# Two buffers for layer 1's x, another interleaving of the last two periods, a flag in two parts, and early recurrent gate products in the last unit

## The reference

```python
# layer 0
mask = adj > 0
h  = relu((x @ W1a)[:, :, None, :] + (x[:, :, None, :] - x[:, None, :, :]) @ W1b + b1)
y  = einsum('bjkh,bjk->bjh', h, mask) @ W2 + mask.sum(-1)[..., None] * b2
x  = layernorm(x + y)
# layer 1
m   = relu(relu(x @ W1 + b1) @ W2 + b2)
msg = relu(einsum('bij,bjh->bih', adj, m))
gi, gh = msg @ W_ih.T + b_ih, x @ W_hh.T + b_hh      # parts r, z, n
r, z = sigmoid(i_r + h_r), sigmoid(i_z + h_z)
n   = tanh(i_n + r * h_n)
out = layernorm(x + (1 - z) * n + z * x)
```

## Time and profile before

| of the profiled execution | |
|---|---|
| its own time | 1053.67 us |
| span, first to last instruction | 1051.9 us |
| TensorE matmuls busy | 903.9 us, 86% |
| VectorE busy | 860.2 us, 82% |
| ScalarE busy | 558.1 us, 53% |
| GpSimd busy | 299.2 us, 28% |
| mean granted TensorE clock | 0.956 |

### The profile page before, as it was taken

The page is one execution under the profiler, slowest core; times in us unless marked ns, Lnnn a source line. Parts: engine busy times, 40 slices in busy tenths (PEclk is TensorE's granted clock), DMA queues, the critical chain, the costliest instruction groups (busy, mean ns, idle before and its releaser), DMA issues.

```text
span 1051.9 us, 24844 instructions
## 1 busy us (share of the span) xinstructions
PE 903.9 (86%) x10037; PEld 609.8 (58%) x10070; DVE 860.2 (82%) x1043; ACT 558.1 (53%) x1612; POOL 299.2 (28%) x285
## 2 busy tenths in 40 slices
PE   2778889989898998989898998989899898997854
PEld 1445656656666666556666665566666655664543
DVE  5489998888988889898889988898888989897531
ACT  3434454665655566564656566564556657453431
POOL 2111120423314151422315152331415142233230
PEclk9799999999999999999999999999999999999875
DMA  3131212112131211122121311213121212110000
GB/s 124 28 95 41 71 42 72 32 36 71 41 82 30 77 41 44 54 51 71 41 66 42 81 39 28 71 41 82 34 73 42 64 34 51 41 42 12 11 11 11
DMA packets 31425, 53.27 MB, mean 51 GB/s; under 512 B 8137, under 2 KB 16972, under 8 KB 31308
## 3 DMA queue, kind: packets, MB, share of 16 engines
q1 hardware_dynamic: 31308, 51.65, 19.1%
HBM read 13.87 MB, written 4.19 MB: 17 GB/s over the span
## 4 chain that ended last, share of the span: by engine, by line
PE 55%; ACT 16%; DVE 12%; issue 8%; POOL 4%; SPq 2%; another core or an unknown queue 1%; DMA 0%; POOLq 0%; DVEq 0%; ACTq 0%
PE PS L735 12%; PE PS L744 8%; DVE AC L1046 5%; PE PS L818 3%; ACT AM L1311 3%; PE PS L583 3%; PE PS L801 3%; DVE AC L1057 3%; PE PS L588 3%; ACT YO L1272 2%; POOL st L1417 2%; PE PS L609 2%; ACT AC L1358 2%; PE PS L721 2%; PE PS L575 2%
## 5 line engine op out<-in xcount | busy, mean ns | idle before, releaser
L1057 DVE SCALAR_TENSOR_TENSOR AC<-PS,AC 128x1152 f32<-128x1152 f32 (+1 forms) x288 | 351.7, 1221 | 79.9 <-PE PS L735 75.8
L1046 DVE SCALAR_TENSOR_TENSOR AC<-PS,AC 128x1152 f32<-128x1152 f32 (+1 forms) x288 | 351.2, 1220 | 66.5 <-PE PS L744 47.2
L735 PE MATMUL PS<-DM,VA 128*128 128x192 fp8e5 (+1 forms) x1152 | 136.8, 243 | 21.9 <-ACT AC L1358 8.4
L735 PE MATMUL PS<-DM,VB 128*128 128x192 fp8e5 (+1 forms) x1152 | 137.8, 244 | 0.0
L744 PE MATMUL PS<-DM,VB 128*64 128x192 fp8e5 (+1 forms) x1152 | 97.7, 250 | 41.7 <-DVE AC L1057 41.7
L735 PEld LDWEIGHTS PS<-DM,VA 128*128 128x128 f16 x1152 | 90.2, 100 | 54.4 <-issue 28.6
L744 PEld LDWEIGHTS PS<-DM,VB 128*64 128x64 f16 x1152 | 43.2, 110 | 119.6 <-issue 62.4
L1468 POOL MEMSET AC<- 128x768 f32 x32 | 23.7, 740 | 282.1 <-DVE DM L1027 267.3
L744 PE MATMUL PS<-DM,VA 128*64 128x192 fp8e5 (+1 forms) x1152 | 99.4, 254 | 0.0
L735 PEld LDWEIGHTS PS<-DM,VB 128*128 128x128 f16 x1152 | 76.9, 99 | 37.9 <-issue 2.6
L1475 POOL TENSOR_TENSOR AC<-AC,NNB 128x512 f32<-128x512 f32 x64 | 70.8, 1126 | 70.4 <-ACT AC L1358 60.2
(11 more groups left out here) (205 smaller groups left out, 1883.1 us busy)
## 6 DMA issues: line engine op xcount, KB each, us to landing
CW<-WM SPq DMA_DIRECT2D x128, 160.0 KB, 2.9
AT<-in_adjt SPq DMA_DIRECT2D x16, 512.0 KB, 4.2
VA<-VN SPq DMA_DIRECT2D x64, 96.0 KB, 2.2
VB<-VN SPq DMA_DIRECT2D x64, 96.0 KB, 2.2
XN<-in_xn SPq DMA_DIRECT2D x16, 256.0 KB, 4.0
out<-YO SPq DMA_DIRECT2D x15, 256.0 KB, 3.0
cs<-in_cst SPq DMA_DIRECT2D x1, 550.5 KB, 3.6
out<-YO SPq DMA_DIRECT2D x2, 128.0 KB, 1.7
```

Source lines behind the costliest of these rows:

```text
L735: last = e.matmul(PS[:, b + i % 2, 256 * (i // 2) + cols.start:256 * (i // 2) + cols.stop], lhs[:, GRAPH[i], 0:128], d[:, i, :], start=Fal ...
L1046: e.scalar_tensor_tensor(dst, tiles(PS[:, b:b + 3, :])[:, :, cols], 0.0, dst, ALU.max, ALU.add).then_inc(s["sx"], 1)
L1057: e.scalar_tensor_tensor(dst, tiles(PS[:, b:b + 3, :])[:, :, cols], 0.0, dst, ALU.max, ALU.add).then_inc(s["sy"], 1)
```

## The change

Four edits are made.

1. XG becomes XG[0] and XG[1], taken by turns by the units. The copy of unit u waits for `h` of unit u-2 instead of u-1.
2. LAST has other strings, so the steps of periods 31 and 32 come in another order.
3. `flag` is split. Its VectorE part is called in period 32, between b-round 8 and b-round 9; the matmuls and the cast are now `fsum`, called after the tail of quad 31.
4. In unit 16 (u = NG) the three products with BH go to PSUM banks 0, 1 and 2 (which only the rounds used) and are issued one after each of `m1`, `m2`, `msg`; behind them come gate_i(0), gt, gate_in (bank 3), gt_in, gate_i(1). The numbers at which the semaphore `gate` is waited for follow from `gate(u)`.

```diff
 LAST = (
-    ("ted", "d", "tde", "td", "td", "d", "nd", "d", "nd", "d", "nd", "d", "nd", "", "nd", "nd", "nd", "n"),
-    ("td", "ed", "td", "ted", "td", "ed", "nd", "nde", "de", "nd", "nd", "n", "nd", "nd", "nd", "nd", "nd", "n"),
+    ("te", "d", "te", "dt", "t", "dd", "n", "ddn", "d", "nd", "nd", "d", "n", "d", "nd", "d", "n", ""),
+    ("td", "ee", "te", "tdd", "te", "dde", "nd", "nd", "de", "nde", "nde", "nd", "d", "n", "", "n", "dd", "nd"),
 )
+def gate(u):
+    return [4 * u + k for k in ((1, 2, 3, 4) if u < NG else (2, 4, 1, 3))]
...
-        XG = sb("XG", [128, PG, 128])
+        XG = [sb(f"XG{i}", [128, PG, 128]) for i in range(2)]
...
                 bank.give(here[0], sem, u + 1)
+                if u == NG and k:
+                    step(*(("gate_h", 0), ("gate_h", 1), ("gate_hn",))[k - 1], k - 1, [("sy", 9 * NQ)])
                 yield
-            for k in range(2):
+            if u == NG:
+                step("gate_i", 0, 0, [])
+                step("gt", 2, [])
+                step("gate_in", 3, [("sy", 9 * NQ)])
+                step("gt_in", 3, [])
+                step("gate_i", 1, 1, [])
+            for k in range(2 if u < NG else 0):
...
+                    if t == NQ and n == 8:
+                        do("flag")
...
-            here = bank.take()
-            do("flag", *here)
-            bank.give(here[0], "flag", 3)
             link = {"t": tail(NQ - 1), "n": link["n"], "d": link["d"]}
             while link:
                 for c in list(link):
                     if next(link[c], 1):
                         del link[c]
                         if c == "t":
+                            here = bank.take()
+                            do("fsum", *here)
+                            bank.give(here[0], "flag", 3)
                             link = {"l": layer1_steps(do, bank, NG), **link}
...
-                ac.wait_ge(s["h"], p)
-                e.activation(XGf[:, w], PS[:, b, w], ACT.Copy).then_inc(s["xgc"], 1)
+                ac.wait_ge(s["h"], u - 1)
+                e.activation(XGf[u % 2][:, w], PS[:, b, w], ACT.Copy).then_inc(s["xgc"], 1)
```

More of the change, by code:

```diff
@@ L264, in build @@
         PS = ctx.enter_context(nc.psum_tensor("PS", [128, 8, 512], F32))
-        XGf = XG[:].rearrange("p k n -> p (k n)")
+        XGf = [t[:].rearrange("p k n -> p (k n)") for t in XG]
         MSf = MS[:].rearrange("p k n -> p (k n)")
@@ L303, in layer1_steps @@
             yield
-            for name, sem in (("xg", "xgc"), ("m1", "m1c"), ("m2", "m2c"), ("msg", "msc")):
+            for k, (name, sem) in enumerate((("xg", "xgc"), ("m1", "m1c"), ("m2", "m2c"), ("msg", "msc"))):
                 yield from bank.spare()
@@ L317, in layer1_steps @@
                 yield
-            yield from bank.spare()
-            here = bank.take()
[L320 to L337, removed]
+            if u < NG:
+                yield from bank.spare()
+                here = bank.take()
+                step("gate_hn", *here)
+                if not late(u):
+                    bank.give(here[0], "hn", u + 1)
+                yield
+                step("gt", *here)
+                if late(u):
+                    bank.give(here[0], "gt", 2 * u + 1)
+                yield
+                yield from bank.spare()
+                here = bank.take()
+                step("gate_in", *here)
+                if not late(u):
+                    bank.give(here[0], "in", u + 1)
+                yield
+                step("gt_in", *here)
+                if late(u):
+                    bank.give(here[0], "gt", 2 * u + 2)
+                yield
             step("tanh")
@@ L593, in gate_hn @@
                     pe.wait_ge(s[name], v)
-                e.matmul(PS[:, b, w], BH[:, 2, :], XGf[:, w], start=True, stop=True).then_inc(s["gate"], 1)
+                e.matmul(PS[:, b, w], BH[:, 2, :], XGf[u % 2][:, w], start=True, stop=True).then_inc(s["gate"], 1)
             def gate_in(u, b, gates):
@@ L820, in out0_c, with fsum @@
                 last.then_inc(s["o0"], 1)
-            def flag(b, gates):
+            def fsum(b, gates):
                 pe.wait_ge(s["flag"], 2)
@@ L831, in tensor_main @@
                                 "v": v, "v_low": v_low, "surplus": surplus, "seeds": seeds, "round_a": round_a, "round_b": round_b,
-                                "s_ov": s_ov, "out0_a": out0_a, "out0_b": out0_b, "out0_c": out0_c, "flag": flag,
+                                "s_ov": s_ov, "out0_a": out0_a, "out0_b": out0_b, "out0_c": out0_c, "fsum": fsum,
                                 **tensor_layer1(e, pe, s)})
@@ L905, in gt @@
                 if late(u):
-                    ve.wait_ge(s["gate"], 4 * u + 3)
+                    ve.wait_ge(s["gate"], gate(u)[2])
                     ve.wait_ge(s["sig"], 2 * u + 1)
@@ L913, in gt_in @@
                 if late(u):
-                    ve.wait_ge(s["gate"], 4 * u + 4)
+                    ve.wait_ge(s["gate"], gate(u)[3])
                     ve.wait_ge(s["gt"], 2 * u + 1)
@@ L1107, in bias, with flag @@
                 e.tensor_tensor(gbs[:], gb[:, 0:2], gb[:, 3:5], ALU.add).then_inc(s["gbs"], 1)
-            def flag(b, gates):
+            def flag():
                 ve.wait_ge(s["s2"], NG)
@@ L1222, in gate_i @@
                 g, c, w, p = unit(u)
-                ac.wait_ge(s["gate"], 4 * u + k + 1)
+                ac.wait_ge(s["gate"], gate(u)[k])
                 ac.wait_ge(s["gbs"], 1)
@@ L1230, in gate_hn @@
                     return
-                ac.wait_ge(s["gate"], 4 * u + 3)
+                ac.wait_ge(s["gate"], gate(u)[2])
                 ac.wait_ge(s["yt"], 2 * u)
@@ L1237, in gate_in @@
                     return
-                ac.wait_ge(s["gate"], 4 * u + 4)
+                ac.wait_ge(s["gate"], gate(u)[3])
                 ac.wait_ge(s["m2"], u + 1)
```

15 lines of the change are left out of this document (7 added, 8 removed).

## The result

The changed kernel takes 1044.03 us (median of 4 runs, 1038.84 to 1044.92); the kernel before, in the same runs and those shown, 1054.11. The ratio is 0.9886, 95% interval 0.9845 to 0.9927: 1.1% faster. The forecast was 1044.3. The profiled execution took 1044.5 us with a span of 1042.7. In all that follows two slow runs are left out, one of e1 (3918 us) and one of the kernel before in the same group (1916 us).

What follows compares the result with a forecast made beforehand. Neither TensorE nor VectorE bounds throughout: uneven heaps of work with chains of waits between. Gains 3.9 + 7.4 - 1.0 - 1.1 + 0.5 = 9.7 from 1053.67 give 1044.0, plus 0.3 for the median 1044.3; range 1040.5 to 1049.5.

Steps and rivals of the forecast that it cites:

- Step 1: Period 31 up to period 32's SW matmuls: they start at 973.9, 6.95 us earlier than 980.85.
- Its one charge: Period 31: a dgen, switch and another dgen beside GpSimd's gd and h cost 0.6 us in all, bounds 0 to 2.9.
- rival C: Period 31: three VectorE instructions each wait out a whole GpSimd instruction, 2.3 us more, 1046.6; chance 0.08.
- Step 2: Period 32's SW matmuls to the end of unit 14's h: 26.6 us, ending at 1000.5, 3.9 earlier than before.
- rival F: Clock falls to 1.2 GHz before period 32's SW matmuls and stays through its dense file: slower, 1060.7; chance 0.05.
- the mark of being wrong: Period 32: h of unit 14 ending after 1003, against a forecast near 1000.5, would show the forecast wrong.
- rival E: GpSimd's queue and XR behind YO take all; unit 14's h ends about 1004 again, 1050 to 1054 us; chance 0.08.
- Step 3: Unit 14's h to s_ov of quad 31: 4.1 us instead of 11.5, gain 7.4, with 1.0 charged for the clock.
- The charge of 1.0 for a low clock at `s_ov`: Behind unit 14's h: s_ov and some of out0 still at the low clock, 1.0 us, bounds 0 and 5.
- rival B: TensorE keeps 1.2 GHz from unit 14's h to unit 16's m1: 4.4 us more, 1048.7; chance 0.14.
- Step 4: s_ov to m1 of unit 16: XR at +8.35, m1 at +13.5 against old 12.36; net 1.1 us lost, bounds 0 and 2.5.
- Step 5: m1 of unit 16 to the last VectorE instruction, old 16.8: net 0.5 us won, bounds -0.5 and 3.

Runs made afterwards that it cites:

- e1: Kernel before with the two XG buffers alone, old order, flag whole, unit 16's gates late: 1053.51 us, ratio 0.9993 to the kernel before.
- e6: Changed kernel with switch and the two dgens of period 32 issued earlier in period 31: 1041.10 us, ratio 0.9869 to the kernel before.
- e3: Changed kernel with unit 16's recurrent products back beside their message parts: 1045.68 us, ratio 0.9919 to the kernel before.
- e5: Changed kernel with eight idle matmuls added in TensorE's gap before period 32's SW matmuls: 1041.01 us, ratio 0.9866 to the kernel before.
- e7: Changed kernel with GpSimd's period 32 queue reordered, power2 of unit 13 earlier, unit 14's gt before unit 15's power1: 1042.18 us, ratio 0.9871.
- e4: Changed kernel with the flag whole again behind the loop: 1045.19 us, ratio 0.9913 to the kernel before.
- e8: Changed kernel with ScalarE's copy XR of the last quad ahead of unit 14's YO: 1043.08 us, ratio 0.9881 to the kernel before.
- e9: Changed kernel run again, unaltered: 1044.47 us, ratio 0.9894 to the kernel before.
- e10: Changed kernel with the reorderings of e6, e7 and e8 together: 1035.12 us, ratio 0.9810 to the kernel before.
- e2: Kernel before with two XG buffers and the new order; flag whole, unit 16's products not early: 1046.69 us, ratio 0.9927.

## Why the prediction was right, and where its terms were not

**Step 1 held in sum: 6.55 us measured, 6.95 forecast.** The walk along both engines' old durations was good to a few tenths. Its one charge was too small: the two VectorE instructions that met GpSimd's took 1.22 and 1.19 us instead of 0.35 and 0.28 (e6, alone), 1.8 us for which I had taken 0.6. The third, the dgen at 975.09, took 0.35 again, so rival C was about half true. All eight profiles that have this order there have a `switch` of 1.18 or 1.19 beside GpSimd's `h`; in the changed kernel it ends at 975.17, just behind that `h` (975.02). This agrees with the rule of the Trainium skill, page "SBUF — State Buffer", section "SBUF: two separate sides", by which VectorE in a two-port mode and GpSimd exclude each other for a whole instruction.

**Step 2 failed in its size: `h` of unit 14 came 29.6 us behind the SW matmuls, not 26.6.** The queue on GpSimd was as walked (26.96, 26.97 and 26.97 us in e3, e5 and e6 at full clock, and e7 shows that the order there costs 1.9). What its 15.1 us, all at 2.4 GHz, missed is that `switch`, held by GpSimd, leaves TensorE idle for 3.06 us right before it, and the clock falls. It was rival F's mechanism at a fifth of F's price: the low clock was over after some 6 us of full load, as the old dip had been, and did not stay. Of the signs named beforehand this one spoke against the forecast: `h` of unit 14 ended at 1004.86, behind the 1003 given as the mark of being wrong, and no earlier than before, which is what rival E expected. E fell by what came behind it.

**Step 3 held, 4.16 against 4.1.** The last b-round's VectorE instruction ended only at 1005.46, behind `h` and not ahead of it as forecast, but `s_ov` waited for ScalarE's Y, so this cost nothing. The charge of 1.0 for a low clock at `s_ov` was not needed in this profile (1.15). In e4, e8 and e9 it was (1.97, 1.97, 1.98), and e9's stretch to `m1` is 1.3 longer: rival B comes and goes from one execution to the next, at less than the 4.4 I gave it.

**Step 4 held, 0.5 lost against 1.1.** XR starts 7.96 us behind `s_ov` and ends 8.32 behind it (forecast 8.35), held by ScalarE's own queue behind power2, which e8 and e10 confirm by taking it away (10.59 to `m1` in e10).

**Step 5 was mis-sized: 2.56 won, 0.5 forecast.** I subtracted the queueing correctly, `msg` starts 4.07 us behind `m1` as walked (4.1). What was wrong shows at the tanh: it stands 7.68 us behind `m1`, where it was 10.83 and the forecast had 10.3 (by its own terms 9.8, since the reduce that costs 0.5 comes behind it). Behind the tanh 0.6 is lost (6.56 us against 5.97), close to that 0.5. The windows of the changed kernel and of e2 show one cause, the clock:

```profile
1022.00:1025.50 3.50, 3.50 (x11) 2.86 (x12) 1.29 (x4) 0.86 (x2) 0.00 (x0) 0.50 0.00 0
1025.50:1029.00 3.50, 3.26 (x21) 2.36 (x20) 0.48 (x1) 1.06 (x3) 0.00 (x0) 0.99 0.00 0
```
```profile
1022.00:1025.50 3.50, 3.10 (x11) 2.02 (x13) 1.20 (x3) 0.86 (x2) 0.00 (x0) 0.50 0.00 0
1025.50:1029.00 3.50, 3.43 (x14) 2.15 (x12) 0.42 (x1) 0.80 (x3) 0.86 (x2) 0.50 0.00 0
```

Moved beside `m1` and `m2`, the products fill TensorE's waits (3.50 of 3.50 busy, 3.10 in e2), the clock is at 2.4 GHz for `msg` and the gate products behind it, where e2 stays at 1.2 up to 1029, and `msg` takes 0.66 instead of 1.12.

But the larger cause is the place of the products. e3 (first) has them late, e10 (second) early, and both are at 1.2 GHz (granted 0.50) for the first 6 us behind `m1`:

```profile
1015.92 1.22 PE L562 MATMUL PS<-XG,BD 128*128 128x256 f32 x2 [0.47 <-ACT XG L1212]
...
1026.54 0.51 ACT L1255 ACTIVATE GN<-GT,gb 128x256 f32<-128x256 f32 x1 [1.25 <-DVE GT L924]
```
```profile
1011.51 1.22 PE L576 MATMUL PS<-XG,BD 128*128 128x256 f32 x2 [0.69 <-ACT XG L1226]
...
1015.87 1.12 PE L597 MATMUL PS<-AT,M 128*64 128x128 f32 x8
...
1020.21 0.51 ACT L1269 ACTIVATE GN<-GT,gb 128x256 f32<-128x256 f32 x1 [0.30 <-DVE GT L938]
```

The tanh comes 10.62 us behind `m1` in e3 and 8.70 in e10 (8.59 in e7, also with `msg` at 1.12): 1.9 to 2.0 us with no higher clock. In the changed kernel, where the clock is up for `msg`, it comes another 0.9 to 1.0 earlier (7.68), and that is the clock's part. The sum had three products leave the way from MS to the tanh; in the traces four do. The message product of z, too, now stands behind `gt_in`, so that two products stand there instead of six, and from MS to `gt_in` e3 takes 5.51 us and e10 2.71.

So the forecast of 1044.3 was right partly by luck: the start of the span was 1.0 later, step 1 0.4 and step 2 3.0 too short, step 3 0.9, step 4 0.6 and step 5 2.1 too long. Most of this is the clock, which I had priced at the wrong places, and in step 5 also the product that I had not counted.

## What to carry to other kernels

A wait taken away (the second XG buffer) was worth 2.1 us at most, and perhaps nothing, until the instructions queued around it were reordered too, so look at what stands in front on every queue before calling a buffer the bound. Where TensorE alternates between 2.4 and 1.2 GHz, price an order by its gaps as well as by its chain: what makes TensorE idle, and where. Independent products moved into such waits paid twice here, about 2 us by their place and 1 by the clock up to the tanh, and even idle matmuls in one gap paid about 3 us. A forecast that hits the sum says little of its terms: compare them landmark by landmark.

## What the runs showed of the hardware

- An idle stretch of 3.06 us on TensorE was followed by about 6 us at 1.2 GHz in five of the seven profiles that have it (the changed kernel, e2, e4, e7, e9), by a later and shorter fall in e8 (28.54 us from SW to the end of `h`) and by none in e3: 2.6 us between two executions of the same instructions up to there. What decides it is not shown.
- Eight idle 128x512 bf16 matmuls in such a gap made the kernel about 3 us faster.
- A VectorE tensor_scalar of 0.28 or 0.35 us took 1.19 or 1.22 beside a GpSimd tensor_tensor. So did a tensor_tensor with both inputs in SBUF, which the prediction had not looked for: X1's scale in the changed kernel, 1.41 us at 996.17 beside GpSimd's `gt`, and 0.43 at 1020.25 alone.

```profile
996.17 1.41 DVE L916 TENSOR_TENSOR X<-XR,st 128x256 f32<-128x256 f32 x1 [0.97 <-POOL st L1427]
...
1020.25 0.43 DVE L916 TENSOR_TENSOR X<-XR,st 128x256 f32<-128x256 f32 x1 [1.09 <-POOL st L1427]
```
